# Products with V issued in pairs of key blocks, and another order of gelu and its split in the expert loop

## The reference

```python
x = x + tanh(g_xattn) * xattn(ctx, layernorm(x), b, seq_len)   # 16 heads of 32, keys/values from ctx
x = x + tanh(g_ffn)   * ffn(layernorm(x), ...)                 # 8 experts, top 2, gelu, hidden 256
# xattn
logits  = einsum('bhqd,bhkd->bhqk', Q * dh**-0.5, K) + b       # masked beyond seq_len
out     = einsum('bhqk,bhkd->bhqd', softmax(logits), V)
# ffn
gates   = top_2_softmax(cosine(x, centroids) + x @ w_route.T)
h       = gelu(x @ w1[e] + b1[e])
out     = sum_e gates[e] * (h @ w2[e] + b2[e])
```

## Time and profile before

| | |
|---|---|
| profiled execution | 1941.25 us, span 1939.5 us |
| attention at full rate | about 119 to 1300 us |
| expert loop | about 1380 to 1939 us |
| busy in the span | PE 1733.0, DVE 1381.7, ACT 1170.1, POOL 1249.5 us |
| busy in 700 to 1000 us (attention) | PE 293.8, DVE 240.7, ACT 212.4, POOL 201.9 of 300 us |
| busy in 1500 to 1700 us (loop) | PE 182.3, DVE 128.1, ACT 108.0, POOL 152.4 of 200 us |
| granted TensorE clock | full (2.4 GHz) in attention and loop, half (1.2 GHz) for 72 us between them |

### The profile page before, as it was taken

One profiled execution on the slowest core, in us unless ns is written; L12 is line 12 of the kernel. 1 busy time (PEld: TensorE's weight loads), 2 busy tenths in 40 slices (PEclk: granted clock), 3 DMA queues, 4 the chain that ended last, 5 costly groups with the idle time before them and its releaser, 6 DMA issues. The chain is left out here.

```text
span 1939.5 us, 32926 instructions
## 1 busy us (share of the span) xinstructions
PE 1733.0 (89%) x9696; PEld 1039.5 (54%) x9697; DVE 1381.7 (71%) x2983; ACT 1170.1 (60%) x2044; POOL 1249.5 (64%) x1507
## 2 busy tenths in 40 slices
PE   0599999999999999999999999984699989999897
PEld 0244555555555555555555555533477767777775
DVE  5568778878878778788778787733666666665665
ACT  1066677676776776776766767663355555555554
POOL 2057577585675776675766857550577777777776
PEclk9999999999999999999999999995799999999999
DMA  3888899898898998998998979643488787868774
GB/s 111 100 175 168 129 203 160 150 208 145 159 193 160 169 183 139 191 179 132 200 154 159 198 112 188 121 133 97 89 153 148 144 142 139 154 130 148 134 146 65
DMA packets 173069, 291.46 MB, mean 150 GB/s; under 512 B 37983, under 2 KB 42079, under 8 KB 172945
## 3 DMA queue, kind: packets, MB, share of 16 engines
q1 hardware_dynamic: 140016, 222.26, 59.2%
q0 software_dynamic: 32928, 67.68, 20.0%
HBM read 127.09 MB, written 71.63 MB: 102 GB/s over the span
## 5 line engine op out<-in xcount | busy, mean ns | idle before, releaser
L998 DVE TENSOR_REDUCE bank<-bank 128x1 f32<-128x512 f32 x1024 | 696.2, 690 | 256.4 <-PE bank L823 248.2
L714 ACT ACTIVATE prob<-bank 128x512 f32<-128x512 f32 x1024 | 593.0, 597 | 359.1 <-PE bank L811 357.7
L659 POOL TENSOR_TENSOR prob<-prob 128x512 f32<-128x512 f32 x256 | 320.7, 1289 | 325.9 <-PE bank L771 325.9
L811 PE MATMUL bank<-stB,stA 100*128 100x512 f32 x1024 | 477.1, 467 | 19.7 <-ACT prob L714 13.6
L823 PE MATMUL bank<-stA,stB 98*128 98x512 f32 x1024 | 423.6, 416 | 31.7 <-DMA stA<-regrouped_then_w 17.5
L811 PEld LDWEIGHTS bank<-stB,stA 100*128 100x128 f32 x1024 | 193.4, 189 | 253.3 <-ACT prob L714 177.5
L663 POOL TENSOR_TENSOR prob<-prob 128x512 f32<-128x512 f32 x256 | 320.3, 1290 | 0.0
L771 PE MATMUL bank<-prob,vin 128*32 128x512 f32 x2048 | 272.7, 605 | 0.7 <-ACT prob L714 0.7
L1263 POOL DMA_INDIRECT out_dram<-yout,scatter_ids x144 | 226.4, 1572 | 52.6 <-issue 52.0
L1195 PE MATMUL bankb<-w_hi,gelu_parts 128*128 x576 | 199.1, 406 | 47.2 <-DVE gelu_parts L1437 47.2
L823 PEld LDWEIGHTS bank<-stA,stB 98*128 98x128 f32 x1024 | 197.9, 193 | 79.2 <-DVE bank L998 37.1
(11 more groups left out here) (181 smaller groups left out, 2234.1 us busy)
## 6 DMA issues: line engine op xcount, KB each, us to landing
stB<-regrouped_then_w SPq DMA_DIRECT2D x192, 256.0 KB, 5.9
stA<-regrouped_then_w SPq DMA_DIRECT2D x192, 256.0 KB, 6.8
x_k_then_w<-in_x_dram SPq DMA_DIRECT2D x16, 1024.0 KB, 8.2
x_k_then_w<-in_ctx_dram SPq DMA_DIRECT2D x16, 1024.0 KB, 12.5
vin<-in_ctx_dram SPq DMA_DIRECT2D x16, 1024.0 KB, 9.3
xres<-in_x_dram SPq DMA_DIRECT2D x16, 1024.0 KB, 6.9
out_dram<-xres SPq DMA_DIRECT2D x16, 1024.0 KB, 7.5
xn_rows<-xn SPq DMA_DIRECT2D x64, 256.0 KB, 5.4
```

Of the source, the lines that this page charges most:

```text
L659: pool.tensor_tensor(first[:, j, :], first[:, j, :], more[:, j, :], ALU.add).then_inc(s_acc, 1)
L714: act.activation(prob_of(st, 0, u)[:, j, :], psS[j % 2][:, :], ACT.Exp).then_inc(s_exp, 1)
L811: pe.matmul(psS[j % 2][:, :], stA[0:100, g, j, kt * P:(kt + 1) * P], stB[0:100, g, j, :], start=True, stop=True).then_inc(s_qk, 1)
L998: dve.tensor_reduce(mx[:, s // 4, s % 4:s % 4 + 1], psM[s % 2][:, :], AX.X, ALU.max).then_inc(s_mx, 1)
```

## The change

It has two parts.

In attention the products with V are issued two key blocks at a time: blocks 0 and 1 in slot 9, blocks 2 and 3 in slot 2 of the next step; before, one block each in slots 5, 9, 13 and 1. The sums move from slot 2 to slot 5. The 32-column products thus stand in three places of a step (2, 5, 9) instead of five (1, 2, 5, 9, 13). `prob` is used round robin over its four blocks, and the waits of the exponentials follow. The transposes and copies behind them move by a slot or so (MT 5 to 6, DT 7 to 8, OT 9 to 10, XT 10 to 11 on TensorE; the copies of the attention 2 to 3 and of the sums 3 to 6 on ScalarE; VectorE's scaling, addition and statistics one slot later), and SM and TK change places in the bank table.

In the expert loop ScalarE makes the high part of gelu half 0 before gelu half 1, and VectorE makes the low part of half 1 in the next step, after the first two turned parts.

```diff
-TURNS = [("TQ", 3), ("SM", -1), ("TK", 3), ("MT", 1), ("DT", -1), ("OT", -1), ("XT", -5), ("LG", -5)]
+TURNS = [("TQ", 3), ("TK", 3), ("SM", -1), ("MT", 1), ("DT", -1), ("OT", -1), ("XT", -5), ("LG", -5)]
...
-                return prob[:, u if u >= 2 else (st.l + off + u) % 2, :, :]
+                return prob[:, (st.l + off + u) % NT, :, :]
...
-                                act.wait_ge(s_pv, st.count(PV, -1, (2, 1, 3, NT)[u]))
-                                if u in (0, 2):
+                                act.wait_ge(s_pv, st.count(PV, -1, (2, 3, NT, NT)[u]))
+                                if u <= 1:
                                     act.wait_ge(s_acc, st.count(ADDS, -1, ADDS if u else HG))
...
-                        if s == 2 and st.on(-1):
+                        if s == 3 and st.on(-1):
                             act.wait_ge(s_pv, st.count(PV, -1, NT))
...
-                        if s == 3 and st.on(-1):
+                        if s == 6 and st.on(-1):
...
-                        if st.g() == 0 and s in (7, 9, 12, 14) and st.on(4):
-                            normalise_q(st, (7, 9, 12, 14).index(s))
+                        if st.g() == 0 and s in (9, 10, 13, 15) and st.on(4):
+                            normalise_q(st, (9, 10, 13, 15).index(s))
...
-                        if j == 1 and u > 0 and st.on(0):
-                            values(st, 0, u - 1)
-                        if s == 1 and st.on(-1):
-                            values(st, -1, NT - 1)
                         if s == 2 and st.on(-1):
+                            values(st, -1, 2)
+                            values(st, -1, 3)
+                        if s == 9 and st.on(0):
+                            values(st, 0, 0)
+                            values(st, 0, 1)
+                        if s == 5 and st.on(-1):
                             sums(st, -1)
...
-                        if s == 10 and st.on(-1):
+                        if s == 11 and st.on(-1):
                             b, before = turn_of(st, "DT")
...
-                        for m in range(KE):
                             act.wait_ge(f_g, st.front(KE, 0, m + 1))
                             act.activation(hT[:, 0, m, :], gelu[:, m, :], ACT.Copy).then_inc(f_hhi, 1)
...
+                    def gelu_lo(st, off, m):
+
+                        dve.wait_ge(f_hhi, st.front(KE, off, m + 1))
+                        dve.tensor_tensor(hT[:, 1, m, :], gelu[:, m, :], hT[:, 0, m, :].bitcast(F32), ALU.subtract).then_inc(f_hs, 1)
...
                         take_turned(st, 0)
                         take_turned(st, 1)
+                        if not st.first:
+                            gelu_lo(st, -1, 1)
...
-                        for m in range(KE):
-                            dve.wait_ge(f_hhi, st.front(KE, 0, m + 1))
-                            dve.tensor_tensor(hT[:, 1, m, :], gelu[:, m, :], hT[:, 0, m, :].bitcast(F32), ALU.subtract).then_inc(f_hs, 1)
+                        gelu_lo(st, 0, 0)
```

More of the change, by code:

```diff
@@ L716, in step @@
                             evac_turned(st, s // 4)
-                        if s == 6 and st.on(1):
+                        if s == 7 and st.on(1):
                             if st.rnd is not None or st.l >= 0:
@@ L737, in step @@
                             normalise(st)
-                        if s == 11 and st.on(-5):
+                        if s == 12 and st.on(-5):
                             bank, took = take_turn(act, st, "XT")
                             act.activation(xT[:, :, :].rearrange("p k t -> p (k t)"), bank[:, :], ACT.Copy).then_inc(took, 1)
-                        if st.g() == 0 and s in (7, 9, 12, 14) and st.on(4):
-                            normalise_q(st, (7, 9, 12, 14).index(s))
+                        if st.g() == 0 and s in (9, 10, 13, 15) and st.on(4):
+                            normalise_q(st, (9, 10, 13, 15).index(s))
                         if s == 10 and st.g() == 1 and st.on(-6):
@@ L832, in step @@
                             turn_rows(st, s // 3)
-                        if s == 5 and st.on(1):
+                        if s == 6 and st.on(1):
                             pe.wait_ge(s_nm, st.count(2, 1, 2))
@@ L839, in step @@
                             last.then_inc(done, 1)
-                        if s in (7, 9) and st.on(-1):
-                            name, src = ("DT", sumT) if s == 7 else ("OT", attT)
-                            if s == 7:
+                        if s in (8, 10) and st.on(-1):
+                            name, src = ("DT", sumT) if s == 8 else ("OT", attT)
+                            if s == 8:
                                 b, before = turn_of(st, "SM")
@@ L850, in step @@
                             last.then_inc(done, 1)
-                        if s == 10 and st.on(-5):
+                        if s == 11 and st.on(-5):
                             pe.wait_ge(s_xn2, st.count(1, -5, 1))
@@ L1008, in step @@
                             aggregate(st, 2 * (st.g() - 2) + s // 4)
-                        if s == 8 and st.on(-1):
+                        if s == 9 and st.on(-1):
                             bank, took = take_turn(dve, st, "DT")
@@ L1022, in step @@
                             dve.tensor_tensor(heads, heads, each, ALU.mult).then_inc(s_scaled, 1)
-                        if s == 11 and st.on(-1):
+                        if s == 12 and st.on(-1):
                             g, par = st.g(-1), ((st.l - 1) // 4) % 2
@@ L1033, in step @@
                             row_norms(st)
-                        if s in (12, 13) and st.on(-1):
-                            column_stats(st, 2 * (s - 12))
-                        if s == 14 and st.g() == 0 and st.on(-4):
+                        if s in (13, 14) and st.on(-1):
+                            column_stats(st, 2 * (s - 13))
+                        if s == 15 and st.g() == 0 and st.on(-4):
                             row_stats(st)
```

## The result

The changed kernel took 2012.3 us (median of 4 executions, 2011.83 to 2016.05); the kernel before, run beside it, 1939.86. The ratio is 1.0374, with a 95% interval of 1.0349 to 1.0398: 3.7% slower. The profiled execution has a span of 2010.1 us, 70.6 more than before. Attention is read from the first sums to the first product with ones behind it (L885 before, L887 now, in the counting of tokens); it grew from 1220.9 to 1317.1 us, and the first sums come 5.5 later. The loop, from the first scatter of the first block to that of the last, shrank from 527.9 to 499.2 us. So attention gives +102, the loop −29, and the stretch between and the end −2.

What follows compares the result with a forecast made beforehand. TensorE was taken to pace attention with VectorE close behind, and GpSimd's gathers and scatters the expert loop. 1938.4 + 20 (attention) − 34 (loop) = 1924, forecast as 1925 us, range 1900 to 1950.

Steps and rivals of the forecast that it cites:

- +20 us for attention: Attention: the paired V products cost +22 over 15 batches, less 2 for first and last steps; bounds −31 and +32.
- walk: Attention: timed count of VectorE's and TensorE's work from the pair run in slot 9; plain step from 18.65 to 19.02 us.
- the 1.8 us that the walk puts at one L823: Attention: TensorE stalls 1.8 us before L823 number 2, waiting for VectorE's reduce 0, which loses the pairs' gain.
- 1.66: Attention: four steps take 77.44 us against 75.78, before a correction to +1.3.
- −2 for both ends: Attention: the first and last steps, where VectorE has less to do, take 2 us off the cost.
- The other moved waits are covered: Attention: other moved work, such as GpSimd's additions and ScalarE's copies, ends before it is needed, so no cost was added.
- 0.5 us a step: Attention on TensorE: joining V runs saves 0.5 us a step, 31 us over 64 steps, if everybody waits for TensorE.
- The loop, −34 us: Expert loop: waits for gelu parts and yout go, the period falls from 15.08 to 14.1 us over 35 periods.
- Rival B: Expert loop: VectorE's low 1 directly before w_parts holds GpSimd's scatter up; period 14.9, time 1955 us, chance 0.14.
- Rival A: Attention: the pairs gain in full, attention −30 and loop −34, time 1874 us, steps of 18.2, chance 0.08.

Runs made afterwards that it cites:

- the kernel with four runs: The changed kernel with V block 2 back in slot 13, so runs stand in slots 2, 5, 9, 13: 1912.56 us.
- the light reduce: Row-maximum reduce over 256 of 512 columns: 1943.24 us with attention's part of the change alone, 1913.73 us in the kernel before.
- the loaded kernel: Attention as before, loop as changed, each VectorE reduce of slots 12 to 15 done twice: 2077.2 us.

## Why the prediction was wrong

- **The step that failed is the one that wrote +20 us for attention.** Its walk charged every instruction at the duration that it has at 2.4 GHz, so it held only while the clock stays there, and the text never asked. The clock fell three times a batch, and attention cost +102: 2012 us against the forecast 1925. The walk did see that VectorE would pace TensorE in the stretch without a run, and priced it; there was no term and no rival for the clock.
- **The walk itself was right where the clock stayed full.** A few plain steps of the changed kernel have no fall. In one of them, TensorE's runs and its two waits:

```profile
305.01 1.92 PE L784 MATMUL bank<-prob,ones 128*32 128x512 f32 x16
...
309.80 1.92 PE L771 MATMUL bank<-prob,vin 128*32 128x512 f32 x16
...
316.02 1.03 PE L864 MATMUL bank<-routeT,xT 128*128 128x16 f32 x8 [0.25 <-DVE xres L1032]
...
319.65 0.51 PE L823 MATMUL bank<-stA,stB 98*128 98x512 f32 x1 [0.42 <-DVE bank L1000]
320.08 1.92 PE L771 MATMUL bank<-prob,vin 128*32 128x512 f32 x16
...
323.98 1.92 PE L784 MATMUL bank<-prob,ones 128*32 128x512 f32 x16
```

  The step takes 18.97, forecast 19.02; from V run to V run it is 10.28, forecast 10.31. The group 1 step was forecast at 19.84 and is 19.70. Only the place was off: the 1.8 us that the walk puts at one L823 come in parts: 0.25 at the route scores, 0.42 at that product, and the rest, which the trace names as no wait, in products that follow each other more slowly.
- **So what the clock cost can be read off.** The plain steps with one fall of 3.4 us take 19.80 to 19.89, 0.9 more than without. Group 0 was forecast at 19.56 and is 22.46; the changed kernel has no such step without a fall, but the one with the addition a slot earlier has, at 19.66, so its falls cost about 2.8. Together that is 4.5 a batch, beside 1.6 at full clock, where 1.66 was forecast. As an estimate over all steps, 60 to 66 of the 102 us are the clock. The rest is those 1.6 a batch, the first sums, which stand three slots further on and come 5.5 later, and about 5 in the last steps, where the forecast had −2 for both ends. One moved run, V 2 back in slot 13, removed nearly all the half clock in the steps (205.4 to 27.7) and 100 us together.
- **"The other moved waits are covered" was wrong in two places.** The tiles of group 0 were not costed: TQ waits up to 0.9 for the last one, and their old slots gave 15 us back in the kernel with four runs. The route scores' wait for the addition, 22.4 us over the span, was not counted; taking it away mostly moved it, for 11 us.
- **"0.5 us a step" for the pairs on TensorE was near**: 0.40 in a plain step where VectorE has time.
- **The loop, −34 us, was right in mechanism and a little large.** It gave −29 in the span, and −32 alone; the period is 14.26 or 14.16, forecast 14.1. The waits went and came as forecast. Rival B happened in part and without its price: scatters lengthened by 97 ns in the mean, four a block, 0.39 us, and gathers shortened by 98, which gives it back. The long scatters are mostly not those beside w_parts. Of the 144, the 43 that run beside a low part of gelu alone take 1820 ns in the mean, the 26 beside a low part and w_parts 1616, the 75 beside neither 1600.
- The rivals: none had the clock. Rival A's plain step of 18.2 was seen only with the light reduce or with a fourth run.

**What brings the clock down is settled only in part.** Shown: the fall comes behind slots 10 to 15, where the change took a V run away; putting one back removes nearly all falls, doubling products in slots 10 to 13 about half of them, filling slots 15 and 0 none; and waits for a loaded VectorE bring it down with all five runs in place. These are not its condition by themselves:

- the missing run: the loaded kernel falls with all five runs, and without the run in slot 13 the changed kernel's group 1 step and the plain steps with the light reduce don't fall;
- VectorE's arrears: the kernel with the light reduce falls in group 0;
- the route scores' wait: without it the falls stay;
- the longest single wait: the changed kernel's group 1 step has 0.78 and 0.44 without a fall, and the kernel before has, at full clock, this row:

```profile
716.02 0.50 PE L811 MATMUL bank<-stB,stA 100*128 100x512 f32 x1 [0.76 <-ACT prob L714]
```

Nor do the waits of a step tell whether it falls. In the changed kernel the plain steps from 305.01 and from 386.18 both wait 0.25 at the route scores (316.02 and 397.18) and nowhere else longer than 0.1 before the place of the fall; the clock stays full in the first and falls at 398.5 in the second. So the cause of a single fall stays open. Slots 10 to 13 also hold two groups of transposes; no run here changed their number, so their part is open, as is what part the waits have.

## What to carry to other kernels

Read the granted clock before pricing a reordering, and again after it: moving dense work out of a stretch in which TensorE has small waits can halve its clock behind that stretch, here at 4.5 us a batch against 1.6 for all that the new order cost at full clock. Compare steps with a fall and without one in the same trace: that prices the clock. Keep the 32-column runs spread out, and after a join look at the stretch that it empties: of the two joins here the one in slot 9 was worth having, and the one that emptied slot 13 cost 100 us. When instructions move by a slot, list every producer whose cover moves with them, those that come once in four steps too.

## What was not expected of the hardware

- The clock fell to 1.2 GHz in the midst of attention with no wait on TensorE longer than 0.9 us over 400 to 1200 us, and with 95.7% busy time there. There each stretch at 1.2 GHz was 3.4 or 6.8 us long in the changed kernel.
- At that clock the distance from a plain product to the instruction behind it went from 0.23 to 0.42 (760.75 to 760.98, and 769.37 to 769.79), and a run of V pairs from 1.92 to 3.48.
- GpSimd's indirect DMAs can lengthen beside VectorE instructions with both inputs in SBUF, gathers and scatters: in one block of the kernel with low 1 behind w_parts the gather beside w_parts takes 2.14 us, where the others take 1.0. It is not so each time: in the kernel before, the 36 scatters beside a low part took 1548 ns in the mean, the other 106 from 1400 us on 1580. What decides was not found.

```profile
1615.42 1.23 DVE L1420 TENSOR_TENSOR w_parts<-x_k_then_w,w_parts 128x1024 fp32r<-128x1024 f32 x1 [0.26 <-ACT w_parts L1355]
1615.47 2.14 POOL L1233 DMA_INDIRECT rows_in<-xn_rows,gather_ids  x1 [0.15 <-issue]
```
